# Sums over neighbours for the last tiles of points by adding row gathers from DRAM, in passes 3 to 7

## The reference, cut to what matters

```python
idx = _knn_indices(xyz, 8)
for i in range(NUM_BLOCKS):                      # 4
    shortcut = points
    p = _lrelu(points)
    g = _group_point(p, idx_t)                   # the 8 neighbours' features
    c = jnp.einsum('oi,bin->bon', w_center[i], p)
    gn = jnp.einsum('oi,bikn->bokn', w_neighbor[i], g)
    points = (c + gn.sum(axis=2)) / (K + 1.0) + shortcut
```

## Time and profile before

| | |
|---|---|
| Time, median of 3 runs | 721.95 us (719.92 to 722.13) |
| The profiled execution, its own time | 719.64 us |
| Its span, first to last instruction | 717.9 us |
| PE busy | 700.1 us, 98% of the span |
| DVE, ACT, POOL busy | 81%, 48%, 35% |
| Mean granted TensorE clock | 0.995 of full |

### The profile page before, as it was taken

How to read it: one execution, slowest core, us unless ns; L and a number is a source line. 1 busy time by engine, 2 the same in 40 slices (tenths; PEclk the granted TensorE clock), 3 DMA queues, 4 the chain that set the end, 5 groups by cost and what they waited for, 6 DMA issues and landing times.

```text
span 717.9 us, 13047 instructions
## 1 busy us (share of the span) xinstructions
PE 700.1 (98%) x5458; PEld 584.5 (81%) x5458; DVE 580.2 (81%) x863; ACT 348.1 (48%) x529; POOL 250.2 (35%) x216
## 2 busy tenths in 40 slices
PE   6999999999999999999999999999998999999998
PEld 4799899778888887888888888877886887888887
DVE  4699999999699899766789798677677799678831
ACT  6456556448417137766892263383472344223210
POOL 2259757646608237400164083064172000000000
PEclk9999999999999999989999999999999999999999
DMA  9510301100000114554400000000000000100101
GB/s 351 178 3 1 117 1 48 41 29 1 1 1 0 62 41 135 190 166 168 167 31 1 1 0 1 0 1 1 0 1 0 2 1 2 42 35 30 46 31 58
DMA packets 21564, 35.66 MB, mean 50 GB/s; under 512 B 10113, under 2 KB 10369, under 8 KB 21505
## 3 DMA queue, kind: packets, MB, share of 16 engines
q1 hardware_dynamic: 20976, 33.78, 14.1%
q10 hardware_dynamic: 528, 1.05, 0.5%
HBM read 30.50 MB, written 4.33 MB: 49 GB/s over the span
## 4 chain that ended last, share of the span: by engine, by line
PE 77%; DVE 12%; POOL 5%; ACT 4%; issue 2%; DMA 1%; SPq 0%; POOLq 0%; ACTq 0%; DVEq 0%
PE bank L1472 25%; PE bank L1494 6%; PE bank L1496 6%; PE bank L1495 6%; PE bank L1519 5%; PE bank L1581 4%; PE bank L1620 4%; PE bank L1622 4%; PE bank L1383 4%; PE bank L1621 4%; PE bank L1385 4%; PE bank L1384 4%; DVE idx L970 2%; DVE vals L968 2%; POOL pts_l L500 1%
## 5 line engine op out<-in xcount | busy, mean ns | idle before, releaser
L1472 PE MATMUL bank<-nbr,pts_h 128*128 128x512 f32 x512 | 203.5, 397 | 4.0 <-DVE pts_l L997 3.9
L1472 PE MATMUL bank<-nbr,pts_l 128*128 128x512 f32 x512 | 200.8, 392 | 0.0
L495 POOL TENSOR_TENSOR p_second<-p_first,p_second 128x512 f32<-128x512 f32 x58 | 77.2, 1335 | 196.1 <-ACT p_second L705 196.1
L1472 PEld LDWEIGHTS bank<-nbr,pts_h 128*128 128x128 f32 x512 | 97.1, 190 | 26.3 <-DVE pts_l L997 4.5
L1472 PEld LDWEIGHTS bank<-nbr,pts_l 128*128 128x128 f32 x512 | 97.0, 190 | 19.9 <-issue 0.2
L718 ACT CAST pts_h<-bank 128x512 fp32r<-128x512 f32 x64 | 37.0, 588 | 155.4 <-PE bank L1472 155.2
L1494 PE MATMUL bank<-wT,pts_h 128*128 128x512 f32 x256 | 101.6, 397 | 0.0
L1496 PE MATMUL bank<-wT,pts_l 128*128 128x512 f32 x256 | 99.8, 390 | 0.0
L1495 PE MATMUL bank<-wT,pts_h 128*128 128x512 f32 x256 | 99.7, 389 | 0.0
L997 DVE TENSOR_TENSOR pts_l<-bank,pts_h 128x512 fp32r<-128x512 f32 x64 | 43.7, 685 | 48.3 <-ACT pts_h L718 47.9
L500 POOL TENSOR_TENSOR pts_l<-p_second,pts_h 128x512 fp32r<-128x512 f32 x58 | 79.1, 1370 | 2.0 <-ACT pts_h L711 2.0
(11 more groups left out here) (212 smaller groups left out, 1341.0 us busy)
## 6 DMA issues: line engine op xcount, KB each, us to landing
more<-a_rows SPq DMA_DIRECT2D x17, 480.0 KB, 4.7
scratch<-a_rows SPq DMA_DIRECT2D x15, 480.0 KB, 4.7
X<-in_ctx SPq DMA_DIRECT2D x12, 512.0 KB, 6.0
out_dram<-X SPq DMA_DIRECT2D x15, 256.0 KB, 2.0
more<-in_ctx SPq DMA_DIRECT2D x4, 512.0 KB, 5.5
X<-in_x SPq DMA_DIRECT2D x2, 1024.0 KB, 5.9
X<-in_x SPq DMA_DIRECT2D x1, 1536.0 KB, 6.8
w_raw<-in_fside_BxSxS SPq DMA_DIRECT2D x1, 1024.0 KB, 11.4
```

Source lines behind the costliest of these rows:

```text
L495: pool.tensor_tensor(p, a, b, ALU.subtract).then_inc(s_p32, 1)
L1472: mm = pe.matmul(bank[u % 3][:], p[:, m, t * P:(t + 1) * P], nbr[b][:, m, hf * HALF:(hf + 1) * HALF], start=(m == 0 and part_ == 0), stop= ...
```

## The change

In passes 3 to 7 the last one or two tiles of points get q in another way. p of the pass is also stored to DRAM row by row (`p_d`), eight tiles of 256 KB. For a gathered tile, SP copies the tile's own p rows into a sum buffer, and POOL issues 8 indirect DMAs that each fetch one neighbour's row (2 KB) for each of the 128 points and add it to the buffer. Passes 3 and 7 gather two tiles with one buffer each (16 gathers that alternate between the buffers), passes 4 to 6 one tile with two buffers that take turns and are added on POOL at the end (8 gathers and one addition). PE then transposes the sum (4 transposes of 128 x 128) before `wp` of the tile that is two before, ACT and DVE split it into high and low part. The second half's units of `aggregate` shrink from 512 columns to 384 or 256.

The gathers stand on POOL at the start of a pass, ahead of the joins for the next pass. `p_low` of a tile waits until its p is stored (and copied, for a gathered tile), and comes one place later in POOL's order. One of the seven broadcast buffers is given up for the sums, and `aT` moves so that `idx` stays whole.

```diff
-        NB = 7
+        NB = 6
...
+        SUMS = {3: ((0,), (1,)), 4: ((0, 1),), 5: ((0, 1),), 6: ((0, 1),), 7: ((0,), (1,))}
+        G_FIRST = min(SUMS)
+        sums = [more[:, 3 - i // 2, i % 2 * HALF:(i % 2 + 1) * HALF] for i in range(4)]
...
+        def gathered_at(it, m):
+            return m + 2 - (NT - gathered(it))
...
+            def store_p(n):
+                it, m = n // NT, n % NT
+                sp.wait_ge(s_p32, n + 1)
+                sp.dma_start(p_d[it % B][m * P:(m + 1) * P, :], p_second[:, m, 0:HALF]).then_inc(s_pd[m], 16)
+                e = m - NT + gathered(it)
+                if e >= 0:
+                    if tiles_gathered(it):
+                        sp.wait_ge(s_gt, tiles_gathered(it))
+                    i, count = own_landed(it, e)
+                    sp.dma_start(sums[i], p_second[:, m, 0:HALF]).then_inc(s_own[i], 16)
+            STORE_AT = {3: range(3), 6: (3, 4), 8: (5,), 10: (6,), 12: (7,)}
...
             def p_low(n):
-                m = n % NT
+                it, m = n // NT, n % NT
                 pool.wait_ge(s_p0, n + 1)
+                if it >= G_FIRST:
+                    pool.wait_ge(s_pd[m], 16 * (it - G_FIRST + 1))
+                    e = m - NT + gathered(it)
+                    if e >= 0:
+                        i, count = own_landed(it, e)
+                        pool.wait_ge(s_own[i], 16 * count)
...
+            def gather(it, e, n):
+                T = it % B * NT + NT - gathered(it) + e
+                i, count = landed(it, e, n)
+                if n == 0:
+                    pool.wait_ge(s_own[i], 16 * own_landed(it, e)[1])
+                elif n < len(SUMS[it][e]):
+                    if joined(it, -1):
+                        pool.wait_ge(s_join, joined(it, -1))
+                else:
+                    pool.wait_ge(s_sum[i], 16 * (count - 1))
+                first = i != SUMS[it][e][0] and n < len(SUMS[it][e])
+                pool.indirect_dma_start(out=sums[i], out_offset=None, in_=p_d[it % B],
+                                        in_offset=bass.IndirectOffsetOnAxis(ap=idx[:, T, n:n + 1], axis=0),
+                                        compute_op=ALU.bypass if first else ALU.add).then_inc(s_sum[i], 16)
+            def gathers(it):
+                for m in range(NT):
+                    pool.wait_ge(s_pd[m], 16 * (it - G_FIRST + 1))
+                for n in range(K0):
+                    for e in range(gathered(it)):
+                        gather(it, e, n)
...
             for it in range(ITS):
+                if it in SUMS:
+                    gathers(it)
...
                         p_join(n)
-                        if n % (2 * CT):
-                            p_low(n - 1)
-                        if n % (2 * CT) == 2 * CT - 1:
-                            p_low(n)
+                        behind = 2 if it + 1 >= G_FIRST else 1
+                        if n % NT >= behind:
+                            p_low(n - behind)
+                        if n % NT == NT - 1:
+                            for k in range(n - behind + 1, n + 1):
+                                p_low(k)
...
+            def gathered_q_high(it, e):
+                act.wait_ge(s_gt, tiles_gathered(it) + e + 1)
+                m = CT - gathered(it) + e
+                act.copy(q_h[:, CT:2 * CT, m * P:(m + 1) * P],
+                         turned_bank(it, e)[:].rearrange("p (t n) -> p t n", t=CT)).then_inc(s_gqh, 1)
...
-                            mm = pe.matmul(bank[u % 3][:], p[:, m, t * P:(t + 1) * P],
-                                           nbr[b][:, m, hf * HALF:(hf + 1) * HALF],
+                            mm = pe.matmul(bank[u % 3][:, 0:w], p[:, m, t * P:(t + 1) * P],
+                                           nbr[b][:, m, hf * HALF:hf * HALF + w],
...
+                if m >= NT - gathered(it):
+                    pe.wait_ge(s_gql, tiles_gathered(it) + m - NT + gathered(it) + 1)
...
+                for t in range(CT):
+                    mm = pe.transpose(turned_bank(it, e)[:, t * P:(t + 1) * P], sums[of[0]][:, t * P:(t + 1) * P],
+                                      ident[:])
+                mm.then_inc(s_gt, 1)
```

More of the change, by code:

```diff
@@ L110, in build @@
         more = sb("more", [P, 4, N], F32)
+        p_d = [nc.dram_tensor(f"p_rows{i}", [N, C], F32, kind="Internal").ap() for i in range(B)]
         a_rows = nc.dram_tensor("a_rows", [CHUNKS, P, P], BF16, kind="Internal").ap()
@@ L145, in build @@
         pick = scratch[:, 2012:2372].rearrange("p (k j r) -> p k j r", k=KH, j=3)
-        bc = [scratch[:, 2372 + 960 * i:3332 + 960 * i].bitcast(BF16) for i in range(3)]             + [more[:, i, 0:960].bitcast(BF16) for i in range(4)]
+        bc = [scratch[:, 2372 + 960 * i:3332 + 960 * i].bitcast(BF16) for i in range(3)]             + [more[:, i, 0:960].bitcast(BF16) for i in range(3)]
         att32 = scratch[:, 2400:2912].rearrange("p (t k) -> p t k", t=TILES)
@@ L184, in parts, with gathered, tiles_gathered, landed @@
             return p_first[:, m, 0:HALF], p_second[:, m, 0:HALF], p_second[:, m, 0:HALF]
+        SUMS = {3: ((0,), (1,)), 4: ((0, 1),), 5: ((0, 1),), 6: ((0, 1),), 7: ((0,), (1,))}
+        G_FIRST = min(SUMS)
+        sums = [more[:, 3 - i // 2, i % 2 * HALF:(i % 2 + 1) * HALF] for i in range(4)]
+        def gathered(it):
+            return len(SUMS.get(it, ()))
+        def tiles_gathered(it):
+            return sum(gathered(i) for i in range(it))
+        def landed(it, e, n):
+            of = SUMS[it][e]
+            i = of[n % len(of)]
+            return i, sum(K0 // len(t) for q in SUMS if q < it for t in SUMS[q] if i in t) + n // len(of) + 1
+        def own_landed(it, e):
+            i = SUMS[it][e][0]
+            return i, sum(t[0] == i for q in SUMS if q <= it for t in SUMS[q])
+        def joined(it, e):
+            return sum(len(t) > 1 for q in SUMS if q < it for t in SUMS[q]) + sum(len(t) > 1 for t in SUMS[it][:e + 1])
         def slots(a, n=1):
@@ L235, in build @@
         s_m = sem("agg_done")
+        s_pd = [sem(f"p_rows_stored{i}") for i in range(NT)]
+        s_sum = [sem(f"rows_landed{i}") for i in range(4)]
+        s_own = [sem(f"own_rows_copied{i}") for i in range(4)]
+        s_join = sem("sums_joined")
+        s_gt = sem("gathered_q_turned")
+        s_gqh = sem("gathered_q_high_ready")
+        s_gql = sem("gathered_q_low_ready")
         s_xu = sem("x_updated")
@@ L381, in _ @@
                     u = 2 * CH * c + t
+                    for m in STORE_AT.get(u, ()):
+                        store_p(NT * G_FIRST + m)
                     if u == 0:
@@ L396, in _ @@
                                  .to_broadcast([P, KH * P])).then_inc(s_bc[u % NB], 16)
+            for n in range(NT * (G_FIRST + 1), NT * ITS):
+                store_p(n)
             for T in range(TILES):
@@ L904, in _ @@
                             p_high(n)
+                    if 0 <= gathered_at(it, m) < gathered(it):
+                        gathered_q_high(it, gathered_at(it, m))
                     side(16 * it + NT + m)
@@ L1458, in aggregate @@
                 b, hf = it % B, j // CT
+                w = HALF - hf * gathered(it) * P
                 if it < B and j % CT == 0:
```

36 lines of the change are left out of this document (33 added, 3 removed).

## The result

The forecast was 706 us, 701 to 718. The changed kernel takes 724.51 us (median of 20 runs, 718.94 to 730.06), the kernel before 721.02 in the same comparison (20 runs, 719.84 to 722.13): a ratio of 1.0049, 95% interval 1.0027 to 1.007. It is slower, by about half a per cent, and the forecast of 15 us gained is wrong in sign. Its runs also lie 11 us apart, those of before 2.3.

What follows compares the result with a forecast made beforehand. PE, 98% busy, was taken as the bound. Gains of 5.5, 2.75, 1.7, 2.75 and 5.2 us in passes 3 to 7, less 2 for DVE, gave 16: 719.64 to 703.6, plus 2.3 for the median, 706 us; range 701 to 718.

Steps and rivals of the forecast that it cites:

- The room in pass 3: POOL's idle gap before pass 3's joins: 8R = 34 us of gathers fit into 43 us, so are hidden.
- R: Round from a gather's issue until the next on the same buffer may go: taken as 4.2 us, upper bound 6.0.
- Pass 3's gain of 5.5 us: Pass 3 on PE: 6.85 us of columns spared, less 0.9 for transposes and 0.5 for SP's later queue.
- a few tenths at most: Passes 3, 4 and 6: cost of the gathered tile's own-row copy, issued second, to the low part, in us.
- Pass 7's 5.2 us: Pass 7's gain: 6.85 us of columns less 0.4 in the units and 1.2 on DVE; room 40.6 us allows R = 5.0.
- Passes 4 to 6: Gains of 2.75, 1.7 and 2.75 us from 384-column matmuls, after transposes and, in pass 5, a 1.5 us wait.
- the cover: All 56 gathers hidden behind the units at R = 4.2, with idle time left before POOL's joins; ends at R = 5.
- A: Rival: gathers somewhat late, R between 5 and 6.2, delaying joins and pass 7's transposes; 715 us at 5.7; chance 0.12.
- B: Rival: POOL's gathers hold DVE up by 5 us or some more, R under 5; 709 to 713 us; chance 0.09.
- the 2 us that I took for it: Allowance for gathers holding DVE up in pass 7's attention parts and pass 3's one-hots; 5 us as bad end.
- C: Rival: descriptor work slowed beside busy DVE makes POOL set the pace; 735 us at R = 7; chance 0.13.
- D: Rival: one more half-clock stretch on PE, in pass 3, costs about 3 us: 709 us; included in the forecast's 0.62.

Runs made afterwards that it cites:

- the four buffers: Against the version with one gathered tile in each of passes 4 to 7: four sum buffers instead of two in passes 4 and 5; 712.15 us, ratio to before 0.9887.

## Why the prediction was wrong

**The room in pass 3** is the step that failed, where the prediction says "Pass 3 needs 8R = 34 us of a gap of 52.7 - 6.9 - 3 = 43" and from it that all gathers are hidden. It took there the round of a quiet pass, and the gathers' time on the DMA engines was no term at all, though the row of DMA shares (0.4 to 0.5 in pass 3) and the window at 309 (share 0.92) showed how busy they were. Measured are rounds of 7.4 and 7.8 us there, so that a chain takes 52 to 55 us and more where 43 were free, and 1.75 us of all 16 DMA engines for a gather: 23.5 + 21 us of 48 with the broadcasts. Halving the gathers, or the price of each, brought the pass back from 95.7 to 84.6 and 84.2 us; keeping all the rest and leaving out the gathers cost about 1 us. So it is shown that the gathers, by their number and their price, cost the 10 us, and the chain of the run with pass 3 alone shows the way over POOL and ACT to PE. That the DMA load is what stretches a round is argued from the shares. PE's 10.8 us of additional idle time and 17.1 us more at half clock, less some 6 us of columns spared, make up the loss in the profile (a stretch at half clock costs at most half its length, and the two overlap in part); which cause has which part was not tested, nor how much of it the late one-hots of DVE make (11.2 us of waiting for broadcasts in 305 to 395, before none).

**The price of a round** was too low as well: "I take R = 4.2 us" against 5.1 in quiet passes and 5.4 to 6 in pass 7. The transfer was sized right: 3.6 us for twice the bytes, measured 3.5 from the end of the issue to the landing. What was short is POOL's part, "something", 0.6 us, where the issue takes 1.54. This alone would not have turned the sign: at R = 5.1 pass 3 would have needed 41 of its 43 us, and by the prediction's own terms passes 6 and 7 would have lost about 1 us.

**Pass 3's gain of 5.5 us** would not have come with shorter rounds either: with one tile, or with cheap gathers, the pass is 84 to 85 us, as without any. PE's freed columns there go into other waits, above all for the last low part (m = 7 starts at 306.7, before at 304.1). The term "a few tenths at most" for the copy of the tile's own rows was too small: POOL waits 4.0 us for it, and PE 3.2.

**Pass 7's 5.2 us** failed by its own condition, R = 5.0: the chains took 43 to 49 us of a room of 40.6. Where the rounds were short, in the run without addition, the pass took 175.0 us, 4.5 below before. So the columns, DVE's share and the units were sized nearly right. The changed kernel's profile is 2.7 us above that run: 1.2 at the late rows, and 1.4 in the third unit, at half clock. The second has no term in the prediction, and it isn't the gathers' alone: the version with passes 4 to 6 only has such a stretch at 544.2 to 547.6 too.

**Passes 4 to 6** were right: 2.75 + 1.7 + 2.75 = 7.2, measured 7.2 (6.8 to 9.0 by the ratio) with gathers there alone. The columns pay as read. PE after, 384 columns, then pass 5's wait for the gathered q:

```profile
409.56 0.33 PE L1596 MATMUL bank<-nbr,pts_h 128*128 128x384 f32 x1
...
412.33 0.33 PE L1596 MATMUL bank<-nbr,pts_h 128*128 128x384 f32 x1
```

```profile
488.64 0.47 PE L1620 MATMUL bank<-wT,pts_h 128*128 128x512 f32 x1 [2.00 <-DVE pts_l L1116]
```

Sixteen in 2.77 us are 0.173 each, forecast 0.177; the wait is 2.0 us, forecast 1.5. But the cover that I gave as the reason was not there: the joins came late, and that cost only tenths, as the four buffers show. In this the 7.2 us were luck.

**The rivals.** A (R 5 to 6.2, 715 us) describes passes 4 to 7, but its price for passes 4 to 6 did not come due. B, DVE held by POOL: the update of x takes 688 ns on average in 540 to 606 after, 680 before (x8 each), the attention part's subtraction 668 against 669 (x4); the 2 us that I took for it are not seen, and neither is more. C, the slower one, put long rounds down to POOL's descriptor work beside a busy DVE. In the quiet window of pass 4 a gather cost POOL 1.54 us with DVE busy 36 of 40 us, and R was 5.1, not 6.7; the sign was C's, the mechanism in the main not. Only in pass 7 is a part of it seen, in issues that take up to 2.65 us, once 3.52; what stretches those was not tested. The Trainium skill (page "SBUF — State Buffer", section "SBUF: two separate sides") gives 0.62 us for a DMA issued by GpSimd alone and 3.1 beside a VectorE copy. POOL's issue of a gather, which need not be the same time, measures 0.96 us without and 1.55 with the addition, nearly throughout passes 3 to 6, with DVE busy. D, another stretch at half clock: besides what was there before there were two more in pass 3, at 337 to 347 and at 368 to 375, the latter from within PE's long wait on, and the one in pass 7.

A sum of the parts run alone, each against the kernel before of its own comparison, closes: 9.7 (pass 3) - 7.2 (passes 4 to 6) + 0.9 (pass 7) = +3.4 us; measured +3.5.

## What to carry over

A transfer that is hidden by one engine's idle time must also fit into the DMA engines' time: price it in both, and add up the share of all that runs beside it, stage by stage, before a chain of dependent transfers is laid there. An in-order queue turns one late operand into a wait for everything behind it, so follow what else stands behind the waiting instruction (here the one-hots behind ACT's high part). A chain of eight rounds multiplies each error in a round by eight; use it only where its room exceeds the upper bound, not the likely value.

## What the hardware showed that I had not expected

A gather of 128 rows of 2 KB with addition costs 1.55 us of POOL, some 3.5 us more until it has landed, and 1.75 us of all 16 DMA engines (the mean of 56, three of which don't add); without addition 0.96, 2.6 and 0.93. The packets go from 80 to 141 for each. Beside broadcasts that take half the DMA engines a round stretches from 5.1 to over 7 us. And the same program of pass 7, with two gathered tiles, took 177.8 to 185.6 us in five profiles, according to how its chains of gathers ran and to the clock, where the versions without gathers in pass 7 have 179.5 to 181.0.
